# Three edits to the order of work in an attention and expert kernel: context halves, the first weight, the gate products

## The chip, the cores and the metric

The kernel runs on one core of one Trainium2 chip. The metric is the device time of one execution in microseconds (us), lower being better. The engines are named as the profile names them: PE is TensorE (matmuls; its weight loads are PEld), DVE is VectorE, ACT is ScalarE, POOL is GpSimd, and SP is the engine that issues nearly all DMAs. Each works through its own list in order and waits on semaphores.

## What is computed

The reference is cross attention followed by a layer of experts, each with a residual:

```python
x = x + _L0_xattn_ref(_layernorm(x, axis=-1), ctx_2048, ...)
x = x + _L0_ffn_ref(_layernorm(x, axis=-1), ...)
```

x is 4 batches of 512 rows of 512 numbers, and the context is 4 batches of 1601 rows of 512 (257 image rows and 1344 text rows, each kind with its own key and value weights). The attention has 16 heads of 32:

```python
q = rms_norm(linear(x, q_w, q_b), norm_q_w)
k = rms_norm(linear(ctx_txt, k_w, k_b), norm_k_w)
v = linear(ctx_txt, v_w, v_b)
k_img = rms_norm(linear(ctx_img, k_img_w, k_img_b), norm_k_img_w)
v_img = linear(ctx_img, v_img_w, v_img_b)
out = attention(q, k_img, v_img) + attention(q, k, v)
return linear(out, o_w, o_b)
```

The second part routes each of 2048 tokens to 4 of 32 experts and adds a shared gated layer, `silu(x @ shared_gate.T) * (x @ shared_up.T) @ shared_down.T`.

## The kernel before, in words

The order of every engine's list is written by hand, one block of code for each engine. There are two programs in a row: the attention, and then the feed-forward part. All engines meet between them.

**Precision.** Matmuls of the projections work on halves: a number of 32 bits is stored as a high half (a 16-bit copy) and a low half (the rest). Three products (high by high, high by low, low by high) make one `product` (line 900), which is 4 chunks by 3 = 12 matmuls of 512 columns. For the context tile k, ACT makes the high half (`ctx_high`, line 493) and DVE the low half (`ctx_low`, line 634). For a weight, ACT makes the high half (`weight_high`, line 489) and DVE the low one (`weight_low`, line 629), each in one instruction over 2048 columns. The semaphores `c_lo` and `w_lo` tell PE that they are there.

**A batch.** Each of the 4 batches has a projection stage of 17 slots (`project`: 13 context tiles for keys and values, 4 tiles of x for queries) and an attention stage of 52 steps. In slot i PE does the key (or query) product of tile i, transposes the normalised key of slot i - 2 (`turn_keys`), and does the value product of tile i - 1. DVE takes the key out of PSUM (`key_raw`, line 648), ACT squares it and sums (`key_square`, line 511), POOL makes the scale (`key_scale`), DVE normalises (`key_norm`, line 661), and ACT and DVE split it (`key_high`, `key_low`). The end of a batch is folded into the projection of the next one. In slots 1 to 4 PE spreads the reciprocal of the softmax sums over the heads (`spread`, line 975, into the banks NUM and DEN) and DVE multiplies with it (`weigh`, line 699); after that come the output product and the norm of the rows of the batch before.

**The change of batch.** PE does the key and the value product of tile 0 of the next batch (`key(bb + 1, 0)`, `value(bb + 1, 0)`), then the last sums of the softmax (`text_part`, line 1118, semaphore `a_den`). DVE has taken out key 0 by then, waits for `a_den` and computes the reciprocal (line 827, semaphore `a_rcp`). Only then does it go into the slots of the next batch, where the low half of context tile 1 stands first. SP waits for `a_den` before it loads x, two residual tiles and then context tile 2.

**The start.** SP first issues the image key weight WKI, context tile 0, the image value weight WVI, context tile 1, two vectors, the text weights WK and WV, and two more vectors. ACT and DVE split WKI, then tile 0, and then WVI; PE begins when all this but WVI is there.

**The end of the attention program.** After the last batch PE waits for the reciprocal and spreads it for head group 0 (line 1176). DVE sums up the reciprocals, PE adds the sum over the rows (line 1188), and DVE sets a flag (line 890) that says whether an exact second pass (never taken with these inputs) is needed. Every engine reads the flag and branches. Then the feed-forward program begins. Its PE list (from line 1811) starts with `spread` for groups 1 to 3, `gate_up(0)` (the gate product and the up product, 12 matmuls each, of the first block of normed rows, x2t[0]), `gate_up(1)`, and the four output products of the last batch. SP has begun to load x2t[0], [1] and [2] after the last scores (line 346, semaphores `s_turned`).

The names `wts`, `hl`, `raw`, `rcp`, `sel`, `x2t`, `sg` and `su` in the rows are weights in halves, context in halves, context as loaded, the reciprocal, the spreading matrices, the normed rows turned, and the shared gate and up weights. Rows of a DMA stand under the line of the call that issues it.

## Time and profile before

| | us |
|---|---|
| median of 3 runs | 1297.05 (1296.89 to 1299.68) |
| the profiled execution | 1295.91 |
| its span in the trace | 1294.1 |
| PE busy | 1203.9 (93%) |
| DVE busy | 865.9 (67%) |
| ACT busy | 676.7 (52%) |
| POOL busy | 186.6 (14%) |

The attention program takes the first 921 us and the feed-forward program the rest. The busy shares are a mean over stages: in most of the span PE works without a gap, and what an edit is worth is read at the places where PE doesn't. A timeline row gives the start and the time in us, the engine, the line, the operation, out<-in, the shapes and the count; the brackets behind it give the idle time of the engine just before and what ended it. A matmul of 32-bit operands (the spreading) leaves two records for one instruction. Starts of matmuls that follow on each other are closer than their durations, so a row of many ends a little later than the next one begins; times of stretches are taken from start to start.

### The profile page before, as it was taken

How to read it: one execution, taken by the hardware profiler on the slowest of the kernel's cores; microseconds unless marked ns; L12 is line 12 of the kernel's file. 1: busy time of each engine (PE TensorE's matmuls, PEld its weight loads, DVE VectorE, ACT ScalarE, POOL GpSimd, SP SyncE). 2: the span in 40 equal slices, each digit the busy share in tenths (PEclk: the TensorE clock that was granted, in tenths of full speed). 3: DMA queues.
4: the chain of work that ended last, by engine and by line, in shares of the span. 5: the costliest groups of instructions: out<-in, count | busy, mean ns of one | idle time of the engine just before them, and what ended most of it. 6: DMA issues, size and time to landing. Idle time of an engine off the chain costs nothing. (4 is left out here: it accounts for less than half of the span.)

```text
span 1294.1 us, 22341 instructions
## 1 busy us (share of the span) xinstructions
PE 1203.9 (93%) x9252; PEld 462.7 (36%) x9252; DVE 865.9 (67%) x1102; ACT 676.7 (52%) x944; POOL 186.6 (14%) x299
## 2 busy tenths in 40 slices
PE   5998999899899989989998998999799999999996
PEld 2543222355322234532223454222254434333332
DVE  6775888787588878758887885899658963122111
ACT  4546998345699924568993455899231111111121
POOL 0210000123000003300000230000120001333342
PEclk9999999899999989999999999999799999999999
DMA  8200000213100021210002123010561325999832
GB/s 301 85 25 18 2 2 2 90 33 108 41 2 2 2 85 39 90 58 2 2 2 82 36 95 139 2 34 2 200 261 66 123 82 201 364 309 304 262 68 30
DMA packets 38398, 117.95 MB, mean 91 GB/s; under 512 B 6544, under 2 KB 6800, under 8 KB 33040
## 3 DMA queue, kind: packets, MB, share of 16 engines
q1 hardware_dynamic: 33168, 105.60, 22.8%
q0 software_dynamic: 5120, 10.82, 4.6%
q8 instruction: 76, 1.25, 0.4%
q14 instruction: 34, 0.28, 0.1%
HBM read 95.67 MB, written 20.73 MB: 90 GB/s over the span
## 5 line engine op out<-in xcount | busy, mean ns | idle before, releaser
L597 ACT ACTIVATE work<-ps 128x1024 f32<-128x1024 f32 (+1 forms) x416 | 403.2, 1021 | 45.2 <-PE ps L1080 41.5
L1086 PE MATMUL ps<-work,vals 128*32 128x512 f32 (+2 forms) x1664 | 221.0, 603 | 0.9 <-ACT work L597 0.6
L903 PE MATMUL ps<-wts,work 128*128 128x512 f16 x864 | 203.7, 388 | 12.1 <-DVE work L636 12.1
L1080 PE MATMUL ps<-quer,keys 32*128 32x512 f16 x2496 | 171.9, 377 | 23.3 <-ACT work L597 9.3
L818 DVE TENSOR_TENSOR work<-work 128x2048 f32<-128x2048 f32 x64 | 146.6, 2291 | 6.0
L818 DVE TENSOR_TENSOR attn<-attn,work 128x2048 f32<-128x2048 f32 x62 | 142.0, 2291 | 5.2
L903 PEld LDWEIGHTS ps<-wts,work 128*128 128x128 f16 x864 | 83.7, 99 | 112.1 <-DVE work L636 14.8
L903 PE MATMUL ps<-wts,hl 128*128 128x512 f16 x480 | 111.9, 385 | 11.4 <-DVE hl L636 11.2
L1880 PE MATMUL ps<-wring,xgt 128*80 128x512 f32 x256 | 114.9, 592 | 0.0
L1080 PEld LDWEIGHTS ps<-quer,keys 32*128 32x128 f16 x2496 | 46.3, 92 | 191.6 <-ACT work L597 166.7
L1706 DVE COPY xgt<-ps 128x320 f32<-128x320 f32 x32 | 15.7, 492 | 138.4 <-PE ps L1871 138.4
L435 POOL TENSOR_SCALAR small<-small 128x1 f32<-128x1 f32 x68 | 13.7, 202 | 614.2 <-ACT work L514 614.2
L514 ACT ACTIVATE work<-work 128x512 f32<-128x512 f32 x68 | 42.9, 631 | 110.2 <-DVE work L653 110.2
L666 DVE SCALAR_TENSOR_TENSOR work<-work,small,vec 128x512 f32<-128x512 f32 (+1 forms) x72 | 63.6, 883 | 43.7 <-POOL small L438 43.6
L509 ACT CAST work<-work 128x512 f16<-128x512 f32 x68 | 42.1, 619 | 79.7 <-DVE work L666 79.7
L1453 ACT ACTIVATE yf<-ps,xg 80x512 f32<-80x512 f32 x32 | 21.9, 684 | 115.3 <-DMA out<-yf,idx 92.2
L1895 PE MATMUL ps<-wring,ht 128*80 128x512 f32 x128 | 62.2, 608 | 10.7 <-ACT ht L1448 8.9
L903 PEld LDWEIGHTS ps<-wts,hl 128*128 128x128 f16 x480 | 46.2, 99 | 68.1 <-issue 19.0
L802 DVE COPY nums<-ps 128x512 f32<-128x512 f32 x16 | 11.1, 692 | 81.0 <-PE ps L1086 81.0
L1086 PEld LDWEIGHTS ps<-work,vals 128*32 128x32 f32 (+2 forms) x1664 | 34.3, 107 | 85.7 <-issue 81.2
L1374 POOL DMA_INDIRECT out<-yf,idx x32 | 45.6, 1424 | 133.0 <-DMA out<-yf,idx 84.7
L1880 PEld LDWEIGHTS ps<-wring,xgt 128*80 128x80 f32 x256 | 38.4, 150 | 71.1 <-issue 70.9
(219 smaller groups left out, 1515.8 us busy)
## 6 DMA issues: line engine op xcount, KB each, us to landing
wring<-in_wx SPq DMA_DIRECT2D x32, 1536.0 KB, 8.9
raw<-in_ctx SPq DMA_DIRECT2D x52, 256.0 KB, 2.8
work<-in_x SPq DMA_DIRECT2D x4, 1024.0 KB, 5.6
table<-nums SPq DMA_DIRECT2D x16, 256.0 KB, 2.3
work<-in_x SPq DMA_DIRECT2D x12, 256.0 KB, 4.4
x<-work SPq DMA_DIRECT2D x12, 256.0 KB, 2.0
x2t_rows<-nums SPq DMA_DIRECT2D x12, 256.0 KB, 2.4
x2t<-x2t_rows SPq DMA_DIRECT2D x3, 1024.0 KB, 7.8
```

What stands on the lines that cost most here:

```text
L509: act.copy(stack[i % 2][:, 0, :], kraw[i % 2]).then_inc(k_hi, 1)
L514: act.activation(junk, kraw[i % 2], ACT.Square, accum_out=ssq[i % 2]).then_inc(k_sq, 1)
L597: act.activation(prob[0:rows, s % PROBS, 2 * half:2 * half + 2, :], ps[0:rows, 2 * pair:2 * pair + 2, :], ACT.Exp, scale=SCALE).then_inc(a ...
L666: ins = dve.scalar_tensor_tensor(kraw[i % 2][a:z, :], kraw[i % 2][a:z, :], rin[i % 2][a:z, :], vec[a:z, weight, :], ALU.mult, ALU.mult)
L818: dve.tensor_tensor(acc, acc, cur, ALU.add).then_inc(a_sum, 1)
L903: mm = pe.matmul(out, lhs(a, c)[:, cols], wts[:, w, z, c * D:(c + 1) * D], start=(k == 0), stop=(k == len(steps) - 1))
L1080: mm = pe.matmul(ps[:, 2 * pair + h % 2, :], k[h * HD:(h + 1) * HD, :], q[h * HD:(h + 1) * HD, :], start=(e == 0), stop=(e == len(terms) - 1))
L1086: return pe.matmul(ps[h * HD:(h + 1) * HD, NUM, :], vals[a:z, ORDER[n], g * P + h * HD:g * P + (h + 1) * HD], prob[a:z, s % PROBS, h, :], ...
L1374: pool.indirect_dma_start(out=out[:, :], out_offset=bass.IndirectOffsetOnAxis(ap=idx[:, n:n + 1], axis=0), in_=yf[n % 2][:, :], in_offset= ...
L1453: act.activation(yf[n % 2][:, :], ps[0:CAP, 2 + n % 2, :], ACT.Copy, scale=xg[n % GATHERS][:, D + n:D + n + 1]).then_inc(m_yf, 1)
L1880: mm = pe.matmul(ps[0:CAP, 7 if n % 2 == 0 else 0, :], xgt[n % 2][:, c, :], wring[n % RING][:, c * D:(c + 1) * D], start=(c == 0), stop=(c ...
L1895: mm = pe.matmul(ps[0:CAP, 2 + n % 2, :], ht[n % 2][:, c, :], wring[n % RING][:, (NC + c) * D:(NC + c + 1) * D], start=(c == 0), stop=(c = ...
```

## The change

**At each change of batch.** The low half of context tile 1 of the next batch is made by DVE before it waits for `a_den` and computes the reciprocal, and not after it. SP loads context tile 2 as soon as the low half of tile 0 is made, before it waits for `a_den`, and not behind the loads of x and the residuals. In slot 0 the load of tile 2 and in DVE's list the low half of tile 1 are left out accordingly.

**At the start.** SP issues context tile 0 ahead of WKI. ACT and DVE split tile 0 first and then WKI in two pieces of 1024 columns; PE waits for the first piece before its first product and for the second one half way through it. For the first batch, ACT makes the high half of context tile 2 right behind that of WK, ahead of the first `key_square` and of WV, and DVE makes the low half behind the first `key_raw`, ahead of WV. Before, both stood in slot 1.

**At the end of the attention.** The 12 gate products of `gate_up(0)` move from the feed-forward program to the place between the last `text_part` and the wait for the reciprocal. Their result stays in bank 0, so the spreading uses other banks, the third spread of the feed-forward program waits for the first `weigh`, and the flag's sum goes to bank 2.

```diff
-SEL_BANK = [(0, 2), (1, 3), (4, 5), (6, 7)]
+SEL_BANK = [(4, 5), (1, 3), (6, 7), (4, 5)]
+GATE_BANK, FLAG_BANK = 0, 2
...
             def one_pass(p):
+                load_ctx(p * B, 0, 0)
                 load_weight(WKI)
-                load_ctx(p * B, 0, 0)
                 load_weight(WVI)
...
                 for bb, b in passes(p):
+                    if b > 0:
+                        sp.wait_ge(c_lo, kvn(bb, 0))
+                        load_ctx(bb, b, 2)
                     upto(sp, a_den, bb * NG)
...
-                        if k is not None and k + 1 < KT:
+                        if k is not None and k + 1 < KT and (b == 0 or k > 1):
                             sp.wait_ge(c_lo, kvn(bb, k - 1))
                             load_ctx(bb, b, k + 1)
...
+            def first_weight_high(p):
+
+                act.wait_ge(s_w[WKI], 16 * (p + 1))
+                for half in range(2):
+                    cols = slice(half * 2 * D, (half + 1) * 2 * D)
+                    act.activation(wts[:, WKI, 0, cols], wstage[WKI][:, cols], ACT.Copy, scale=WS).then_inc(w_hi, 1)
+
...
-                    if i + 1 in KV_AT:
+                    if i + 1 in KV_AT and (b > 0 or i != 1):
                         ctx_high(bb, KV_AT[i + 1])
...
                     if b == 0 and i == 0:
                         weight_high(p, WK)
+                        ctx_high(bb, 2)
...
                     if b == 0:
-                        weight_high(p, WKI)
                         ctx_high(bb, 0)
+                        first_weight_high(p)
                         weight_high(p, WVI)
...
-                    if i + 1 in KV_AT:
+                    if i + 1 in KV_AT and i != (0 if b > 0 else 1):
                         ctx_low(bb, KV_AT[i + 1])
...
                     if b == 0 and i == 0:
+                        ctx_low(bb, 2)
                         weight_low(p, WV)
...
                 if b + 1 < B:
                     key_raw(bb + 1, 0)
+                    ctx_low(bb + 1, 1)
                 dve.wait_ge(a_den, (bb + 1) * NG)
...
             def product(out, lhs, w, cols=slice(0, P), halfway=None):
                 steps = [(c, a, z) for c in range(NC) for a, z in PARTS]
                 for k, (c, a, z) in enumerate(steps):
+                    if halfway is not None and k == len(steps) // 2:
+                        pe.wait_ge(w_lo, halfway)
...
                 if b == B - 1:
+                    pe.wait_ge(s_turned[0], 16 * (p + 1))
+                    pe.wait_ge(f_wlo, 3 * p + 1)
+                    steps = [(c, a, z) for c in range(NC) for a, z in PARTS]
+                    for k, (c, a, z) in enumerate(steps):
+                        pe.matmul(ps[:, GATE_BANK, :], swt[SG][:, a, c * D:c * D + P], m.x2t[0][:, :, z, c, :],
+                                  start=(k == 0), stop=(k == len(steps) - 1))
                     pe.wait_ge(a_rcp, bb + 1)
...
                 image, text = SEL_BANK[g]
+                if g == 3:
+                    pe.wait_ge(t_mt, 1)
...
-                for w, bank in ((SG, n % 2), (SU, 2 + n % 2)):
+                for w, bank in ((SG, n % 2), (SU, 2 + n % 2))[1 if n == 0 else 0:]:
```

How the lists read at the places of the prediction follows; the words in brackets are the semaphores that a row waits for. DVE at the first change of batch, before:

```order
L818 TENSOR_TENSOR attn<-attn,work 128x2048 [waits a_sum]
L653 SCALAR_TENSOR_TENSOR work<-ps,vec 128x512 [waits k_mm]
L827 RECIPROCAL rcp<-ps 128x512 [waits a_den]
L636 TENSOR_TENSOR work<-raw,work 128x512 [waits c_hi]
L666 SCALAR_TENSOR_TENSOR work<-work,small,vec 128x512 [waits k_rin]
L636 TENSOR_TENSOR work<-raw,work 128x512 [waits c_hi]
L672 TENSOR_TENSOR work<-work 128x512 [waits k_hi]
L653 SCALAR_TENSOR_TENSOR work<-ps,vec 128x512 [waits k_mm]
```

The same place now (the lines have moved: 636 is 660, 666 is 690, 827 is 853):

```order
L843 TENSOR_TENSOR attn<-attn,work 128x2048 [waits a_sum]
L677 SCALAR_TENSOR_TENSOR work<-ps,vec 128x512 [waits k_mm]
L660 TENSOR_TENSOR work<-raw,work 128x512 [waits c_hi]
L853 RECIPROCAL rcp<-ps 128x512 [waits a_den]
L690 SCALAR_TENSOR_TENSOR work<-work,small,vec 128x512 [waits k_rin]
L660 TENSOR_TENSOR work<-raw,work 128x512 [waits c_hi]
L696 TENSOR_TENSOR work<-work 128x512 [waits k_hi]
L677 SCALAR_TENSOR_TENSOR work<-ps,vec 128x512 [waits k_mm]
```

One row has moved from behind the reciprocal to ahead of it. ACT at the start of the program, before (`s_w3` is the arrival of WKI, `s_w4` WVI, `s_w1` WK, `s_w2` WV; `s_raw0` and `s_raw1` are the arrivals of context tiles):

```order
L491 ACTIVATE wts<-nums 128x2048 [waits s_w3]
L496 CAST hl_60<-raw 128x512 [waits s_raw0]
L491 ACTIVATE wts<-nums 128x2048 [waits s_w4]
L496 CAST work<-raw 128x512 [waits s_raw1]
L491 ACTIVATE wts<-quer 128x2048 [waits s_w1]
L514 ACTIVATE work,small<-work 128x512 [waits k_raw]
L491 ACTIVATE wts<-attn 128x2048 [waits s_w2]
L496 CAST work<-raw 128x512 [waits s_raw0]
```

The same place now:

```order
L511 CAST hl_60<-raw 128x512 [waits s_raw0]
L502 ACTIVATE wts<-nums 128x1024 [waits s_w3]
L502 ACTIVATE wts<-nums 128x1024
L506 ACTIVATE wts<-nums 128x2048 [waits s_w4]
L511 CAST work<-raw 128x512 [waits s_raw1]
L506 ACTIVATE wts<-quer 128x2048 [waits s_w1]
L511 CAST work<-raw 128x512 [waits s_raw0]
L529 ACTIVATE work,small<-work 128x512 [waits k_raw]
L506 ACTIVATE wts<-attn 128x2048 [waits s_w2]
```

The first weight is in two rows behind tile 0, and the cast of tile 2, which waits for its own load, stands ahead of the square (line 514, now 529) and of WV. PE at the end of the attention program, before:

```order
L1121 MATMUL ps<-attn,ones 32x512 [waits a_sum]
L1121 MATMUL ps<-attn,ones 32x512 x3
L1176 MATMUL ps<-rcp,sel 128x512 [waits a_rcp]
L1176 MATMUL ps<-rcp,sel 128x512
L1188 MATMUL ps<-small 1x1 [waits f_chk]
```

The same place now:

```order
L1150 MATMUL ps<-attn,ones 32x512 [waits a_sum]
L1150 MATMUL ps<-attn,ones 32x512 x3
L1207 MATMUL ps<-x2t_76,sg 128x512 [waits f_wlo,s_turned0]
L1207 MATMUL ps<-x2t_76,sg 128x512 x11
L1211 MATMUL ps<-rcp,sel 128x512 [waits a_rcp]
L1211 MATMUL ps<-rcp,sel 128x512
L1223 MATMUL ps<-small 1x1 [waits f_chk]
```

Twelve matmuls stand where PE had only a wait; the feed-forward program has twelve less ahead of its first up product.

## Rows read from the trace of the kernel before

**Rows 1.** Timeline of PE, DVE and ACT around the first change of batch.

```profile
216.10 0.69 DVE L636 TENSOR_TENSOR hl<-raw,hl 128x512 f16<-128x512 f32 x1
...
230.60 3.36 DVE L827 RECIPROCAL rcp<-ps 128x512 f32<-128x512 f32 x1 [1.02 <-PE ps L1121]
...
233.88 0.63 DVE L636 TENSOR_TENSOR work<-raw,work 128x512 f16<-128x512 f32 x1
...
234.56 5.30 PE L903 MATMUL ps<-wts,work 128*128 128x512 f16 x12 [4.03 <-DVE work L636]
238.14 0.62 ACT L496 CAST work<-raw 128x512 f16<-128x512 f32 x1 [7.80 <-DMA raw<-in_ctx]
...
241.93 2.78 PE L912 MATMUL ps<-wts,work 128*64 128x512 f16 x24
...
249.60 0.69 DVE L702 TENSOR_TENSOR nums<-nums,ps 128x512 f32<-128x512 f32 x1 [1.35 <-PE ps L983]
```

**Rows 2.** Busy times by window: engines in order, then granted clock, DMA share, GB/s.

```profile
234.60:242.00 7.40, 7.40 (x18) 2.76 (x20) 2.46 (x4) 2.42 (x6) 0.38 (x2) 0.60 0.58 206
```

**Rows 3.** Timeline: the second and third change of batch.

```profile
460.23 3.36 DVE L827 RECIPROCAL rcp<-ps 128x512 f32<-128x512 f32 x1 [1.02 <-PE ps L1121]
...
469.27 1.88 PE L983 MATMUL ps<-rcp,sel 128*128 128x512 f32 x4
...
471.08 2.78 PE L912 MATMUL ps<-wts,work 128*64 128x512 f16 x24
...
689.39 3.36 DVE L827 RECIPROCAL rcp<-ps 128x512 f32<-128x512 f32 x1 [1.02 <-PE ps L1121]
...
699.45 2.78 PE L912 MATMUL ps<-wts,work 128*64 128x512 f16 x24
```

**Rows 4.** Timeline of PE: the first scores after the first and second change.

```profile
340.78 0.83 PE L1080 MATMUL ps<-quer,keys 32*128 32x512 f16 x12 [0.21 <-ACT vals L504]
...
569.94 0.83 PE L1080 MATMUL ps<-quer,keys 32*128 32x512 f16 x12 [0.21 <-ACT vals L504]
```

**Rows 5.** DMA issues at 5.45 us and 10.58 us: size, us to landing.

```profile
vec<-in_kw SPq DMA_DIRECT2D x1, 256.0 KB, 14.0
...
raw<-in_ctx SPq DMA_DIRECT2D x1, 256.0 KB, 9.6
```

**Rows 6.** Timeline of ACT at the start, and of PE at 75 us.

```profile
19.05 0.63 ACT L514 ACTIVATE work<-work 128x512 f32<-128x512 f32 x1 [2.96 <-DVE work L653]
...
19.68 1.90 ACT L491 ACTIVATE wts<-attn 128x2048 f16<-128x2048 f32 x1
...
75.08 0.61 PE L962 MATMUL ps<-ident,work 128*128 128x128 f16 x8 [1.71 <-DVE keys L683]
```

**Rows 7.** Waits of DVE from 20 to 76 us: total, times, longest.

```profile
DVE work L666 <- POOL small L438: 9.3, 8, 1.7
DVE wts L631 <- ACT wts L491: 2.6, 1, 2.6
DVE work L672 <- ACT work L509: 1.4, 2, 0.7
```

**Rows 8.** DMA issue of x2t[0] at 908.42 us, in the columns of Rows 5.

```profile
x2t<-x2t_rows SPq DMA_DIRECT2D x1, 1024.0 KB, 5.5
```

**Rows 9.** Timeline: the end of the attention and the start of the feed-forward.

```profile
917.08 3.78 PE L1176 MATMUL ps<-rcp,sel 128*128 128x512 f32 x4 [3.48 <-DVE rcp L827]
...
921.02 0.15 DVE L890 TENSOR_SCALAR flag<-ps 1x1 int32<-1x1 f32 x1 [2.10 <-PE ps L1188]
...
926.60 2.05 PE L1738 MATMUL ps<-rcp,sel 128*128 128x512 f32 x2 [5.61 <-PEq L159]
...
933.54 2.75 PE L1733 MATMUL ps<-x2t,sg 128*128 128x512 f16 x12
...
938.75 0.69 DVE L1489 TENSOR_TENSOR attn<-nums,attn 128x512 f16<-128x512 f32 x1
...
943.90 10.52 PE L1733 MATMUL ps<-wts,attn 128*128 128x512 f16 x48
```

More of the change, by code:

```diff
@@ L282, in added, with weights @@
             return (bb * NG + g) * ADDS + a + 1 - PRODUCT_SUMS * (bb // B)
+        def weights(p, k):
+            return 7 * p + k + 1
         def rows_of(n):
@@ L627, in own, with first_weight_low @@
                 return dve_steps[0]
+            def first_weight_low(p):
+                for half in range(2):
+                    cols = slice(half * 2 * D, (half + 1) * 2 * D)
+                    dve.wait_ge(w_hi, 7 * p + half + 1)
+                    dve.scalar_tensor_tensor(wts[:, WKI, 1, cols], wstage[WKI][:, cols], WS, wts[:, WKI, 0, cols],
+                                             ALU.mult, ALU.subtract).then_inc(w_lo, 1)
             def weight_low(p, w):
-                dve.wait_ge(w_hi, 6 * p + W_ORDER.index(w) + 1)
+                dve.wait_ge(w_hi, weights(p, W_ORDER.index(w) + 1))
                 dve.scalar_tensor_tensor(wts[:, w, 1, :], wstage[w], WS, wts[:, w, 0, :], ALU.mult,
@@ L859, in one_pass @@
                     if b == 0:
-                        weight_low(p, WKI)
                         ctx_low(bb, 0)
+                        first_weight_low(p)
                         weight_low(p, WVI)
@@ L889, in _ @@
             dve.wait_ge(f_sum, 1)
-            dve.tensor_scalar(flag[:, :], ps[0:1, XTURN, 0:1], SAFE, 0.0, ALU.is_le, ALU.is_equal).then_inc(f_flag, 1)
+            dve.tensor_scalar(flag[:, :], ps[0:1, FLAG_BANK, 0:1], SAFE, 0.0, ALU.is_le, ALU.is_equal).then_inc(f_flag, 1)
             dve.wait_ge(f_flag, 1)
@@ L898, in _, with product @@
             PARTS = ((0, 0), (0, 1), (1, 0))
-            def product(out, lhs, w, cols=slice(0, P)):
+            def product(out, lhs, w, cols=slice(0, P), halfway=None):
                 steps = [(c, a, z) for c in range(NC) for a, z in PARTS]
                 for k, (c, a, z) in enumerate(steps):
+                    if halfway is not None and k == len(steps) // 2:
+                        pe.wait_ge(w_lo, halfway)
                     mm = pe.matmul(out, lhs(a, c)[:, cols], wts[:, w, z, c * D:(c + 1) * D],
@@ L922, in key @@
                     if bb % B == 0:
[L923 removed]
+                        pe.wait_ge(w_lo, 7 * (bb // B) + 1)
                 if i >= 2:
@@ L937, in key @@
                     if bb % B == 0:
-                        pe.wait_ge(w_lo, 6 * (bb // B) + 3)
+                        pe.wait_ge(w_lo, weights(bb // B, 3))
                     mixed(bank, ctx_lhs(k), WK, WKI).then_inc(k_mm, 1)
                 else:
-                    product(ps[:, bank, :], ctx_lhs(k), WK if k > 2 else WKI).then_inc(k_mm, 1)
+                    product(ps[:, bank, :], ctx_lhs(k), WK if k > 2 else WKI,
+                            halfway=weights(bb // B, 1) if bb % B == 0 and k == 0 else None).then_inc(k_mm, 1)
             def value(bb, k):
@@ L989, in output @@
                     if q == 0:
-                        pe.wait_ge(w_lo, 6)
+                        pe.wait_ge(w_lo, weights(0, 6))
                 if j < 2:
@@ L1187, in _ @@
             pe.wait_ge(f_chk, 2 * B + 2)
-            pe.matmul(ps[0:1, XTURN, 0:1], total, one, start=True, stop=True).then_inc(f_sum, 1)
+            pe.matmul(ps[0:1, FLAG_BANK, 0:1], total, one, start=True, stop=True).then_inc(f_sum, 1)
             pe.wait_ge(f_flag, 1)
```

13 lines of the change are left out of this document (5 added, 8 removed).

## The prediction

> **What bounds the kernel now.** I read the page first (PE busy 93% of the span), then PE's waits stage by stage, and then the timeline where PE stands still. In three of the places that the change touches PE is the engine that everybody waits for, and it loses time there itself: at each change of batch it stands 4.03 us until the low half of context tile 1 is made, which DVE does behind its reciprocal of 3.36 us [rows 1]. The key product behind this wait then takes 234.56 to about 239.7, 5.1 us for 12 matmuls, where the same product on a warm engine takes 2.6 (12 of the 48 gate and up matmuls of rows 9, which run from 933.54 to 943.90, so 0.216 us each). The granted clock says why: its mean is 0.60 from 234.60 to 242.00 [rows 2], mostly the lower level of 1.2 GHz, after PE had been idle. Does time that is won there reach the end? The case has its own test. From the start of the reciprocal to the mixed key product (the first matmuls of slot 2) the first change takes 241.93 - 230.60 = 11.33 us and the second 471.08 - 460.23 = 10.85, 0.48 less [rows 1, 3]. The first scores of these batches come 340.78 - 230.60 = 110.18 and 569.94 - 460.23 = 109.71 after it, 0.47 less [rows 1, 3, 4]. So PE's list carries a gain of slot 2 whole to the attention.
>
> The first batch is another matter. There DVE never waits for PE from 20 to 76 us: its waits are for POOL and ACT alone, links of one chain (square, scale, normalise, split) that it is itself part of [rows 7], and PE waits for that chain, 1.71 us at 75.08 for a key that DVE stores [rows 6]. What delays this chain at its head moves the end; what hastens PE ahead of it doesn't.
>
> **Part 1, the changes of batch.** The low half of tile 1 (0.63 us on DVE) moves into the 1.02 us in which DVE waits for the sums, so it costs nothing; if ACT made the high half later it would delay the reciprocal. PE then does the key product right behind the sums, 2.6 us at full clock, and is done some 0.8 us before the reciprocal. It has the reciprocal 3.36 us after its start, with 0.05 us from engine to engine (DVE ends at 234.51, PE starts at 234.56 [rows 1]). The first spread takes 471.08 - 469.27 = 1.81 us on a warm engine [rows 3]. So the mixed key product can start 3.36 + 0.05 + 1.81 = 5.22 us after the start of the reciprocal. It needs tile 2 by then. Before, tile 2 was loaded behind x and two residuals, and ACT waited 7.80 us for it, until 238.14 [rows 1], 7.5 us after the reciprocal's start; so the moved low half alone would win little, and the earlier load is what the rest hangs on. Now it's loaded once the low half of tile 0 is made, at 216.8 [rows 1], 13.8 us ahead of the reciprocal: SP waits there for tile 0 only, and behind this wait stand only the loads that wait for the sums anyway. The load of tile 3 takes the old place of tile 2 and lands near 238, before DVE wants it at about 239. After the reciprocal DVE normalises key 0 (0.7) and makes the low half of tile 2 (0.65), done some 1.4 us after the reciprocal and 0.4 us before the spread ends. That is the tightest point. Gains: 11.33 - 5.22 = 6.11, 10.85 - 5.22 = 5.63, and for the third change (699.45 - 689.39) - 5.22 = 4.84 [rows 1, 3]. **Sum: 16.6 us.** Bounds: the idle time alone, 3 x (4.03 - 0.8) = 9.7, if the clock still fell; 17.5 if the spread took 1.5.
>
> **What is late next** in these slots is DVE. Before, it waited 1.35 us for the second spread at 249.60, that is 7.67 us after the mixed product began [rows 1]. That wait now ends at 230.60 + 5.22 + 7.67 = 243.5. Between the reciprocal (233.96) and there DVE has 14 operations of 0.63 to 0.74 us [rows 1], at a mean of some 0.65 from start to start 9.1 us, so it is ready at 243.1. It stays ahead by 0.4 us, and PE stays the bound.
>
> **Part 2, the start.** PE can begin about 2 us earlier, as the split of WKI is in pieces and tile 0 is ready before. But PE isn't the bound of the first batch. The chain's head is the square on ACT at 19.05 and then WV's high half at 19.68 [rows 6], on which DVE's low half and all keys behind it hang. Now the cast of tile 2 stands ahead of both, and it waits for its load. That load was issued at 10.58 and took 9.6 us, until 20.2; the vector issued before it, at 5.45, landed at 19.45 [rows 5]. The queue was full, so a load that is issued 4.7 us sooner, but still behind that vector, lands at about the same time. ACT then starts the cast at 20.2 and ends it at 20.85 (0.62 and the hop), and the square, due at 19.05, comes 1.8 us late. DVE's moved low half is off the chain in either place. **Cost: 1.8 us.** Bounds: 0, if the tile lands before WK's high half is done; and a gain of 2.1, PE's earlier start, if I am wrong about the chain.
>
> **Part 3, the end of the attention.** The 12 gate products need x2t[0], issued at 908.42 and there after 5.5 us, at 913.9 [rows 8]. PE is idle from 913.60 (917.08 less 3.48) [rows 9], so they run from about 914.0 to 916.6 under the reciprocal, which ends at 917.0. They take 12 x 0.216 = 2.6 us off the feed-forward's list, where PE runs without a gap from 933.54 to 943.90 and on into the output products [rows 9]. These need DVE's last low half, done at 939.44; PE would come at 941.3, so 1.9 us of cover are left and the gain is whole. The output products start the chain to the next norm, so it passes on. Besides, PE is no longer idle for 3.48 us before the first spread, so that takes 1.81 and not 3.78 us, and ends at 918.9. The flag's sum then waits for DVE, which was ready at 918.92 (921.02 less 2.10) [rows 9], and the flag comes 1.8 us earlier. From flag to feed-forward all engines read, branch and meet (5.61 us of PE's idle time), which just moves. The spread of group 3 waits for a `weigh` that is long done. **Sum: 2.6 + 1.8 = 4.4 us**, bounds 1.8 (the output products wait after all) and 5.
>
> **The sum.** 16.6 + 4.4 - 1.8 = 19.2 us. The profiled execution took 1295.91 us, so it would take 1276.7. The median of the runs lies 1.1 above it, so I forecast 1277.9. The experts at the end hang on the chain before and move with it.
>
> **Rivals.**
> - *Tile 2 lands early at the start.* If the load overtakes the vector, the loss goes: 1276.1, and with a gain of PE's head start 1274. Against it: in rows 5 the tile landed 0.7 us behind the vector, issued 5.1 us before it. The Trainium skill (DMA: Bandwidth & Descriptors, Queues, rings and completion order) says that completion isn't first in, first out for one issuing engine, since data descriptors carry no barrier. By that rule the time would be this rival's; the landings of rows 5 speak for order. Chance 0.14.
> - *DVE becomes the bound at the change of batch.* Its 14 operations have 0.4 us to spare; two of them wait for a half that ACT makes, which can add 0.7 each. Then each change wins 1.0 to 1.4 us less, 3 to 4 in all: 1281 to 1282. Chance 0.12.
> - *The gate products come too late.* If x2t[0] lands after the reciprocal, they stand in front of the spread, at low clock, 12 x 0.43 = 5.1 us. That eats the 4.4 us: about 1282.6. Against it: 913.9 in rows 8. Chance 0.07.
> - *Slower than before.* With the pauses gone, PE would be granted 1.2 GHz in part of the attention stages. Matmuls that took T us at full clock take 2T there. The 19.2 us are gone from T = 19.2, and it decides for slower by more than the margin from T = 22: with 30 us of such matmuls the time is 1277.9 + 30 = 1308. Against it: the clock is below full here only after PE's pauses [rows 2]. Chance 0.02.
> - *It doesn't do what it says:* the moved steps wait for something I missed, and two of the three changes win nothing: 1289. Chance 0.03.
>
> **How the numbers follow.** The forecast has 0.62, from 1275.5 to 1280. The range 1273.5 to 1282.5 takes in the early landing and the DVE rival, 0.88 at face value; each case is itself uncertain by some 2 us (the three runs lie 2.8 apart), which leaves a little over 8 in 10. The measurement tells 0.2%, 2.6 us, from no change. All cases but the slower one and a failure of several parts win more than that: faster 0.96, same 0.02, slower 0.02.
>
> **What would show it.** Right: PE's wait before the key product of tile 1 is gone; the mixed key product starts 5.2 us after each reciprocal; the granted clock stays full there; ACT waits at 16 to 20 us for context tile 2 and WV's high half starts near 21.5; the wait at 75 us is longer by about 2 us; gate products lie under the last reciprocal, and 12 matmuls are missing in the feed-forward. Wrong: DVE's `weigh` no longer waits for PE; WV's high half starts before 20; the first scores of the first batch come earlier, not later.

## The result: 13 us faster, 6 us less than forecast

| | before | changed |
|---|---|---|
| median of 4 runs, us | 1296.97 (1295.46 to 1299.68) | 1284.01 (1282.3 to 1285.85) |
| ratio (95% interval) | 1 | 0.9901 (0.9886 to 0.9916) |
| the profiled execution, us | 1295.91 | 1282.94 |
| its span, us | 1294.1 | 1281.1 |
| PE busy, us | 1203.9 (93%) | 1205.8 (94%) |

The forecast was 1277.9 and its range 1273.5 to 1282.5, so the time lies outside. The sign was right, and the places of the gain were right. A single execution can be slow as a whole, and ratios leave it out; below that is one run, of `d3_start_only` (6833.44 us). I go through the places in the order of the program.

**The changes of batch do what was forecast.** The same stretch as rows 1, in the changed kernel (start, duration, engine, line, operation, count, and idle time before it with what ended it):

```profile
230.09 0.68 DVE L660 TENSOR_TENSOR work<-raw,work 128x512 f16<-128x512 f32 x1
...
231.06 2.76 PE L931 MATMUL ps<-wts,work 128*128 128x512 f16 x12
231.19 3.36 DVE L853 RECIPROCAL rcp<-ps 128x512 f32<-128x512 f32 x1 [0.43 <-PE ps L1150]
...
234.70 1.95 PE L1012 MATMUL ps<-rcp,sel 128*128 128x512 f32 x4 [0.88 <-DVE rcp L853]
...
236.58 2.78 PE L940 MATMUL ps<-wts,work 128*64 128x512 f16 x24
...
244.26 0.69 DVE L726 TENSOR_TENSOR nums<-nums,ps 128x512 f32<-128x512 f32 x1 [1.05 <-PE ps L1012]
```

PE's wait of 4.03 us before the key product is gone; it now stands 0.88 us before the spread, for the reciprocal. The key product takes 2.76 us where it took 5.30, and the mixed product starts 236.58 - 231.19 = 5.39 us after the reciprocal. DVE waits 1.05 us for the second spread, so it isn't the bound. The window of this stretch (busy time of PE, PEld, DVE, ACT and POOL, granted clock, DMA share, GB/s) has the clock at full speed, where rows 2 had 0.60:

```profile
231.00:236.60 5.60, 4.72 (x22) 1.79 (x18) 5.32 (x5) 1.05 (x2) 0.74 (x2) 1.00 0.78 248
```

The first scores come 104.22, 104.23 and 104.23 us after the three reciprocals, against 110.18, 109.71 and 108.92 [rows 1, 3, 4]. That is 5.96 + 5.48 + 4.69 = 16.1 us. The reciprocals of the second and third change in the changed kernel, each with the first scores behind it:

```profile
456.49 3.36 DVE L853 RECIPROCAL rcp<-ps 128x512 f32<-128x512 f32 x1 [0.43 <-PE ps L1150]
...
560.72 0.83 PE L1109 MATMUL ps<-quer,keys 32*128 32x512 f16 x12 [0.21 <-ACT vals L519]
...
681.79 3.36 DVE L853 RECIPROCAL rcp<-ps 128x512 f32<-128x512 f32 x1 [0.43 <-PE ps L1150]
...
786.02 0.83 PE L1109 MATMUL ps<-quer,keys 32*128 32x512 f16 x12 [0.22 <-ACT vals L519]
```

The old times that this is measured from differ a little by trace: three kernels below that keep the old change of batch (c3, d3, d4) have 328.5, 327.4 and 328.4 us for the three together, where the kernel before has 328.8. So up to 1.4 of the 16.1 us can be the luck of one trace.

**The attention stages are longer.** From the first scores of a batch to the start of its reciprocal, behind the last sums, is work that the change doesn't touch (I call it the attention stage). It took 119.45 us for batches 1 and 2 and 115.36 for batch 3 before, and 121.08, 121.07 and 116.97 now: 4.9 us in all. Only batch 0 is unchanged (119.38 and 119.36). The loss is at the head of each stage. PE at the head of batch 1's, first before, then changed:

```profile
342.81 0.83 PE L1080 MATMUL ps<-quer,keys 32*128 32x512 f16 x12 [1.21 <-ACT work L597]
344.77 0.82 PE L1080 MATMUL ps<-quer,keys 32*128 32x512 f16 x12 [1.13 <-ACT work L597]
345.52 1.06 PE L1086 MATMUL ps<-work,vals 128*32 128x512 f32 x8
```

```profile
335.41 0.83 PE L1109 MATMUL ps<-quer,keys 32*128 32x512 f16 x12 [0.21 <-ACT vals L519]
337.45 0.83 PE L1109 MATMUL ps<-quer,keys 32*128 32x512 f16 x12 [1.21 <-ACT work L613]
339.40 1.38 PE L1109 MATMUL ps<-quer,keys 32*128 32x512 f16 x12 [1.13 <-ACT work L613]
340.71 1.94 PE L1115 MATMUL ps<-work,vals 128*32 128x512 f32 x8
```

The pauses are the same in both kernels: PE waits 1.21 and then 1.13 us for ACT's exponentials, since there are no older scores to work on yet. In the changed kernel the granted clock falls behind the second of them, and the same matmuls take longer, the eight of the last row nearly twice as long. The windows of the first 10 us, before and changed, and within the latter of the first 4 and the next 3 us:

```profile
340.78:350.78 10.00, 7.66 (x97) 1.98 (x98) 1.70 (x3) 7.75 (x8) 0.00 (x0) 1.00 0.01 2
```

```profile
335.41:345.41 10.00, 7.67 (x76) 1.97 (x80) 1.70 (x3) 6.69 (x7) 0.00 (x0) 0.83 0.00 1
335.41:339.40 3.99, 1.66 (x24) 0.46 (x25) 1.70 (x3) 3.01 (x4) 0.00 (x0) 1.00 0.01 2
339.40:342.42 3.02, 3.02 (x21) 0.68 (x25) 0.00 (x0) 2.46 (x3) 0.00 (x0) 0.52 0.00 0
```

The mean of 0.83 over 10 us is 3.4 us at the lower level, 1.2 GHz; work at half speed for 3.4 us loses 1.7, and the stages are 1.62 longer. PE's busy share doesn't show this: at the lower clock PE counts as busy. It even rose by 1.9 us in all.

**The start.** ACT, which rows 6 show before:

```profile
19.19 0.62 ACT L511 CAST work<-raw 128x512 f16<-128x512 f32 x1 [3.36 <-DMA raw<-in_ctx]
19.71 0.62 ACT L529 ACTIVATE work<-work 128x512 f32<-128x512 f32 x1
...
20.34 1.90 ACT L506 ACTIVATE wts<-attn 128x2048 f16<-128x2048 f32 x1
```

The cast waits 3.36 us for its load. Of the DMA issues, these are the vector issued at 5.1 us and the tile issued at 5.6 us (size, us to landing), which so landed at 18.4 and 19.1:

```profile
vec<-in_kw SPq DMA_DIRECT2D x1, 256.0 KB, 13.3
...
raw<-in_ctx SPq DMA_DIRECT2D x1, 256.0 KB, 13.5
```

WV's high half starts at 20.34 where it started at 19.68. The first scores of batch 0 come at 111.83, not 111.22: 0.6 us later.

**The end of the attention.** PE and DVE where rows 9 show them before, and first the reciprocal in the kernel before, which rows 9 don't show:

```profile
913.67 3.36 DVE L827 RECIPROCAL rcp<-ps 128x512 f32<-128x512 f32 x1 [0.93 <-PE ps L1121]
```

```profile
902.99 3.36 DVE L853 RECIPROCAL rcp<-ps 128x512 f32<-128x512 f32 x1 [0.93 <-PE ps L1150]
...
903.46 2.76 PE L1207 MATMUL ps<-x2t,sg 128*128 128x512 f16 x12 [0.54 <-DMA x2t<-x2t_rows]
906.40 1.98 PE L1211 MATMUL ps<-rcp,sel 128*128 128x512 f32 x4 [0.18 <-DVE rcp L853]
...
908.54 0.14 DVE L916 TENSOR_SCALAR flag<-ps 1x1 int32<-1x1 f32 x1 [0.29 <-PE ps L1223]
...
914.01 2.05 PE L1775 MATMUL ps<-rcp,sel 128*128 128x512 f32 x2 [5.50 <-PEq L160]
...
922.11 2.75 PE L1768 MATMUL ps<-x2t,su 128*128 128x512 f16 x12
...
929.88 2.32 PE L1768 MATMUL ps<-wts,attn 128*128 128x512 f16 x10
```

From the reciprocal to the flag it takes 908.54 - 902.99 = 5.55 us (7.35 before), to the first spread 5.47 more (5.58), and to the output products 15.87 more (17.30). The last is 1.43 less, not 2.6, because the spreads behind the meeting of the engines run longer at the lower clock. Changed, then before:

```profile
914.01:922.11 8.10, 8.10 (x12) 3.35 (x13) 6.08 (x11) 1.24 (x2) 1.25 (x8) 0.64 0.69 230
```

```profile
926.60:933.54 6.94, 6.94 (x13) 2.91 (x13) 5.15 (x9) 1.24 (x2) 1.25 (x8) 0.75 0.57 188
```

The sum of the trace: 16.1 (changes of batch) - 4.9 (attention stages) - 0.6 (start) + 3.3 (end of the attention) - 1.0 (from the output products to the end, 351.2 us where it was 350.2) = 12.9 us, but for rounding the whole difference of the spans, 13.0. The last term isn't the change's: over all traces of this study this stretch took 349.3 to 354.0 us in the six with the old end of the attention and 349.4 to 352.2 in the eight with the new one. Here too the clock has a part. In the trace of the changed kernel PE waits 1.91 us for ACT in the experts, and the granted clock of the window 1110:1120 is 0.83; in the trace of before it is 1.00 from 943 to 1260.

```profile
1113.42 2.80 PE L1930 MATMUL ps<-wring,ht 128*80 128x512 f32 x4 [1.91 <-ACT ht L1483]
```

### The profile page after: what moved, and what is told of

Its sections match the earlier page's. It is cut to its first block and busy times, and to the rows that moved or that the text cites. A ratio compares the mean times of both kernels' runs of the same rounds, so it can differ in the third digit from the quotient of the medians.

```text
span 1281.1 us, 22343 instructions
## 1 busy us (share of the span) xinstructions
PE 1205.8 (94%) x9252; PEld 461.9 (36%) x9252; DVE 865.3 (68%) x1103; ACT 676.6 (53%) x945; POOL 186.5 (15%) x299
## 5 line engine op out<-in xcount | busy, mean ns | idle before, releaser
L1115 PE MATMUL ps<-work,vals 128*32 128x512 f32 (+2 forms) x1664 | 223.6, 610 | 0.9 <-ACT work L613 0.6
L827 DVE COPY nums<-ps 128x512 f32<-128x512 f32 x16 | 11.1, 691 | 85.9 <-PE ps L1115 85.9
```

Source lines behind the costliest of these rows:

```text
L1115: return pe.matmul(ps[h * HD:(h + 1) * HD, NUM, :], vals[a:z, ORDER[n], g * P + h * HD:g * P + (h + 1) * HD], prob[a:z, s % PROBS, h, :], ...
```

## The experiments

The theory after these traces: the low clock at the head of the attention stages takes back 4.9 us, and comes of the two pauses there. Rivals: the scores are slow for some other reason and the clock only follows; or the difference to the forecast lies in the parts, each worth less than I said.

### The changed kernel again, fillers, and the change of batch alone

`c1_after_again` is the changed kernel once more, to see what repeats.

> The changed kernel once more, for another traced execution. Theory A (TensorE's clock): in the first trace the granted clock fell at the start of the second, third and fourth attention stage, and each took 121.1 us from its first scores to the next reciprocal instead of 119.45. It depends on when PE's pauses of 1.2 us fall, so another execution may show 119.45 in all three (they lie 225.3 us apart and fared alike), and then be about 4.9 us shorter. Theory B (the moved load and half lengthen the attention stage itself, at its end): 121.1 us in every execution at full clock or not. Median 1284 by both.

`c2_after_fill` gives PE work in the two pauses, matmuls whose result is never read (the bank is written anew later):

```diff
+                def keep_busy(n):
+                    for _ in range(n):
+                        pe.matmul(ps[:, NUM, :], ident[:, :], quer[:, 0, 0, :], start=True, stop=True)
+
                 scores(0)
+                if b > 0:
+                    pe.wait_ge(o_out, xn(out_batch(bb - 1), QT - 1))
+                    pe.wait_ge(n_out, xn(out_batch(bb - 1), QT - 1))
+                keep_busy(4)
                 scores(1)
+                keep_busy(4)
```

The two new waits are for readers of that bank.

> The changed kernel with two times 4 extra matmuls of 512 columns (0.216 us each) at the start of each attention stage, into a bank that is overwritten later, where PE waits 1.2 us for ACT behind the first and the second scores. Theory A: the granted clock stays full there, each attention stage takes 119.4 to 119.8 us, and the median falls by 3 to 5 us against the changed kernel, to 1279 to 1281. Theory B: the stages stay at 121.1 us and the median at 1284 or above.

`c3_before_fill` is the kernel before with the same fillers.

> The kernel before with the same extra matmuls. Its trace showed no fall of the clock at any attention start. Theory A: it wins at most 1 to 2 us in the median (where other executions than the traced one had a fall), 1295 to 1297. Theory B: no effect, 1297. If the extra matmuls themselves cost time, this run shows it: each 0.2 us of it 0.8 us in all.

`c4_changes_only` is the kernel before with only the edits at the changes of batch (the low half ahead of the reciprocal, the load ahead of the sums).

> The kernel before with the edits at the changes of batch alone (low half of tile 1 ahead of the reciprocal, tile 2 loaded early); start and end as before. By the prediction 16.6 us less, 1280.4. Theory A: 16.6 less up to 4.9 for the clock at three attention starts, so 1280.4 to 1285.3, and the mixed key product 5.4 us after each reciprocal starts. Theory B: 11.7 less, 1285.3, with attention stages of 121.1 us at full clock.

| | median, us (range, runs) | ratio (95% interval) | stages of batches 0 to 3 in the trace, us |
|---|---|---|---|
| c1_after_again | 1283.77 (1282.4 to 1284.64, 4) | 0.9896 (0.9881 to 0.9911) | 119.39, 119.48, 121.10, 117.01 |
| c2_after_fill | 1278.1 (1277.05 to 1280.33, 4) | 0.9852 (0.9835 to 0.9869) | 119.40, 119.47, 119.47, 115.37 |
| c3_before_fill | 1296.37 (1292.54 to 1299.33, 12) | 0.9985 (0.9972 to 0.9997) | 119.37, 119.45, 119.45, 115.34 |
| c4_changes_only | 1285.87 (1283.38 to 1289.91, 6) | 0.9914 (0.9897 to 0.9930) | 119.37, 121.10, 121.10, 116.98 |

PE at the head of batch 1's attention with fillers, and the window that answers to the one above:

```profile
336.17 1.04 PE L1191 MATMUL ps<-quer,ident 128*128 128x512 f16 x4
337.45 0.83 PE L1109 MATMUL ps<-quer,keys 32*128 32x512 f16 x12 [0.24 <-ACT work L613]
338.21 1.04 PE L1191 MATMUL ps<-quer,ident 128*128 128x512 f16 x4
339.40 0.82 PE L1109 MATMUL ps<-quer,keys 32*128 32x512 f16 x12 [0.16 <-ACT work L613]
340.16 1.07 PE L1115 MATMUL ps<-work,vals 128*32 128x512 f32 x8
...
335.41:345.41 10.00, 9.60 (x104) 2.60 (x105) 1.70 (x3) 7.74 (x8) 0.00 (x0) 1.00 0.01 2
```

The scores start at the same 337.45 and 339.40 as without fillers, since ACT sets these; what changes is the clock behind them. The stages are back at their old length, and the time goes from 1283.8 to 1278.1. Work that nobody needs makes the kernel faster, so the clock is the cause and not the consequence. The gain of 5.7 us in the median is more than the 3 to 5 that I expected and than the stages can give (4.9 at most); the traces of c1 and c2 are 3.7 us apart, 3.3 of it in the two stages that fell in c1. The rest isn't explained, and the intervals allow it to be scatter. On the kernel before, whose stages hadn't fallen in its trace, the fillers are worth 0.15%, just clear of nothing. The change of batch alone brings 11.1 us, about what 16.1 - 4.9 leaves (its median of 1285.87 is 0.6 above the range that I expected), with all three stages after it 1.6 us longer: the loss comes with this part, not with the start or the end.

It isn't certain from one execution to the next, though: c1 has the identical program and kept its stage of batch 1. Over all traces, those of the next sections included:

```
                                            stages traced   of them fallen
changes of batch in full, no fillers              12               8
  (changed kernel twice, c4)          of these, batch 0: 3 traced, 0 fallen
no change or a part of it, no fillers             20               2
  (before, d1, d2, d3, d4)
with fillers (c2, c3, e1, e2, e3, f1)             24               0
                     of these, behind the shortened change: 15 traced, 0 fallen
```

The Trainium skill (TensorE: Matmul & The Clock Gate, A second HAM failure mode: psum-queue depth-cycling) tells of a kernel in which short idle times between groups of matmuls let the clock go down and up again. The traces here agree with it: the clock fell behind pauses of 1.21 and 1.13 us, and never where fillers stood in them. Why the identical pauses fell 8 times of 9 behind the shortened change of batch and seldom in the other kernels, I can't settle. The Trainium skill (TensorE: Matmul & The Clock Gate, What's actually happening) says that the monitor is free-running and isn't reset when a kernel starts; that would fit with c1, but no run here tests it.

### The two halves of the change of batch, apart

`d1_low_half_only`, the kernel before with the one moved DVE step:

```diff
-                    if i + 1 in KV_AT:
+                    if i + 1 in KV_AT and (b == 0 or i > 0):
                         ctx_low(bb, KV_AT[i + 1])
...
                     key_raw(bb + 1, 0)
+                    ctx_low(bb + 1, 1)
                 dve.wait_ge(a_den, (bb + 1) * NG)
```

> The kernel before with the low half of context tile 1 ahead of the reciprocal, and tile 2 loaded where it was. Theory A (both edits are needed, the load is what the rest hangs on): tile 2 still lands 7.5 us after the start of the reciprocal, ACT and DVE split it by 8.9, so the mixed key product starts 8.9 to 9.0 us after it instead of 11.33, 10.85 and 10.06: 5.3 us in all, 1292. Rival: PE's 4.03 us wait was the whole matter, and each change wins 4 us or more: 1285 or less.

`d2_load_only`, with the early load alone:

```diff
+                    if b > 0:
+                        sp.wait_ge(c_lo, kvn(bb, 0))
+                        load_ctx(bb, b, 2)
                     upto(sp, a_den, bb * NG)
...
-                        if k is not None and k + 1 < KT:
+                        if k is not None and k + 1 < KT and (b == 0 or k > 1):
                             sp.wait_ge(c_lo, kvn(bb, k - 1))
                             load_ctx(bb, b, k + 1)
```

> The kernel before with tile 2 loaded early, and the low half of tile 1 behind the reciprocal as before. Theory A: PE still waits 4.0 us and does the key product at the lower clock, and DVE has tile 2 ready before that ends, so the mixed key product starts no earlier than before, 10 to 11.3 us after the reciprocal: 1296 to 1297, no change. Rival: what was won is the load alone, 1290 or less.

Medians 1297.04 and 1297.14 us (10 runs each), ratios 1.0007 (0.9996 to 1.0019) and 1.0007 (0.9994 to 1.0020) to 1296.16 of the kernel before beside them. Neither alone shows a gain; together, in c4, they win 11. PE at the first change in d1, then in d2:

```profile
230.35 2.76 PE L904 MATMUL ps<-wts,work 128*128 128x512 f16 x12
...
239.54 4.08 PE L913 MATMUL ps<-wts,work 128*64 128x512 f16 x23 [3.59 <-DVE work L636]
```

```profile
234.56 4.22 PE L906 MATMUL ps<-wts,work 128*128 128x512 f16 x12 [4.03 <-DVE work L639]
...
240.44 2.78 PE L915 MATMUL ps<-wts,work 128*64 128x512 f16 x24
```

In d1 the pause has only moved: the key product runs at full clock right behind the sums, but then PE stands 3.59 us for the low half of tile 2 (whose load lands as late as in rows 1) and the mixed product takes 4.08 us for 23 matmuls instead of 2.78 for 24. After the first reciprocal the mixed product starts 2.3 us sooner, at 9.05 us as expected, but the first scores come only 0.7 us sooner: most of the gain goes to the low clock in the mixed product. At the second change they come 0.3 us sooner and at the third 0.7 us later. My expectation for d1, 5.3 us and 1292, had left this out and was wrong by 5 us; the one for d2, no change, held. In d2 the old pause of 4.03 is still there, its three changes win 0.8 us together, and one of its four stages fell (121.08). Two waits, one behind the other, both had to go.

### The start alone and the end alone

`d3_start_only` is the kernel before with the edits at the start; `d4_end_only` is the kernel before with the gate products in front of the wait for the last reciprocal, and the banks that go with it. Their diffs are the corresponding hunks of the diff above.

> The kernel before with the three edits at the start alone. Theory A (the first batch hangs on the chain of DVE, ACT and POOL that the cast of tile 2 holds up): the first scores come at 111.8 instead of 111.2, 0.6 us later, as in the changed kernel's traces, though PE starts 2.2 us earlier; time 1297 to 1298. Rival: the head start of PE pays and the first scores come 2 us earlier, 1295.

> The kernel before with the gate products under the last reciprocal, and nothing else changed. By the prediction the four output products start 4.4 us earlier after the last reciprocal's start (30.23 us before, 25.8). The changed kernel showed 26.89, since the granted clock stayed at 1.2 GHz for two more of the spreads of the feed-forward. Theory A: 25.8 to 26.9, by where the clock rises; time 1292.7 to 1294. Rival: the whole 4.4 us are always lost to the clock, no change.

d3 measured 1297.51 us, ratio 1.0005 (0.9992 to 1.0018), as expected, though not by the 0.6 us at the start that I had named. d4 measured 1292.61, ratio 0.9973 (0.9961 to 0.9986), 3.5 us, as expected. ACT at the start of d3:

```profile
20.70 0.62 ACT L508 CAST work<-raw 128x512 f16<-128x512 f32 x1 [4.65 <-DMA raw<-in_ctx]
21.23 0.62 ACT L526 ACTIVATE work<-work 128x512 f32<-128x512 f32 x1
...
21.85 1.89 ACT L503 ACTIVATE wts<-attn 128x2048 f16<-128x2048 f32 x1
```

Here the tile landed at 20.7 and the first scores of batch 0 came at 113.28, 2.06 us later than before. That is the forecast's case. The list of loads is the changed kernel's, where the tile landed at 19.1 (13.5 us from issue to landing there, 15.1 here); in the four traces of the changed kernel with this list and order of halves (the first one, c1, c2, e2) the first scores came at 111.8. In every trace but those of e1 and f1, whose loads stand in another order, the first scores come 91.4 to 91.5 us after WV's high half starts, from 19.54 us in d4 to 21.85 in d3. So the term of the start was right in its mechanism, but its size is set by when this load lands, which differed by 1.6 us; why it landed later in d3, no run shows.

In d4 the last reciprocal to the output products took 26.62 us, 3.6 less than the 30.23 of before, and the stage of batch 0 fell for once (121.02). The end is worth about what the changed kernel showed, 3.3.

### Three edits on top of the fillers

`e1_fill_start`: WK is issued ahead of the two image vectors, and context tile 2 ahead of WV, once its buffer is free.

```diff
                 load_ctx(p * B, 0, 1)
+                load_weight(WK)
                 if p == 0:
                     load_vec(KB + 1, "kib", s_vi)
                     load_vec(KW + 1, "kiw", s_vi)
-                load_weight(WK)
+                sp.wait_ge(c_lo, kvn(p * B, 0))
+                load_ctx(p * B, 0, 2)
                 load_weight(WV)
...
-                        if k is not None and k + 1 < KT and (b == 0 or k > 1):
+                        if k is not None and k + 1 < KT and k > 1:
                             sp.wait_ge(c_lo, kvn(bb, k - 1))
                             load_ctx(bb, b, k + 1)
```

> The changed kernel with the extra matmuls of c2_after_fill, and at the start WK issued ahead of the two image vectors and context tile 2 ahead of WV, behind a wait for the low half of tile 0. If the head of the first batch's chain is the landing of WK (13.9 us) and then the wait for tile 2 (19.2), tile 2 now lands by 15 to 16, WK by 12.5, and the first scores come 2 to 2.5 us before those of the changed kernel (111.8), at 109.3 to 109.8; median 1275.6 to 1276.1 against 1278.1. Rival: WV or the text vectors, now 1 to 2 us later, hold the chain instead, and nothing or less than 0.5 us is won.

`e2_fill_flag`: 24 more such matmuls behind the sum for the flag, which PE works off while it waits for the flag, branches and meets the others.

```diff
+            for _ in range(24):
+                pe.matmul(ps[:, 3, :], ident[:, :], quer[:, 0, 0, :], start=True, stop=True)
             pe.wait_ge(f_flag, 1)
```

> The changed kernel with the extra matmuls of c2_after_fill, and 24 more (5.2 us at full clock) behind the sum for the flag, where PE stands still for 5.5 us between the two programs. If PE reads the flag while they run, the clock stays full in the spreads of the feed-forward, and the output products start 2 to 2.9 us earlier than in c2_after_fill; 1275.5 to 1276. Rival: PE reads the flag and branches only behind them, all engines wait for it, and the kernel is 3 to 5 us slower than c2_after_fill, 1281 to 1283.

`e3_fill_halves_back`: the halves of context tile 2 of the first batch stand in slot 1 again, behind WV, as before the change.

> The changed kernel with the extra matmuls of c2_after_fill, and the high and low half of tile 2 of the first batch back in slot 1, behind WV. Theory A (ACT's wait for that tile ahead of the square costs the 0.6 us): WV's high half starts at about 19.4 instead of 20.3, the first scores come at 110.9 to 111.2 instead of 111.8, and the median falls by 0.6 to 0.9, to about 1277.4. Rival: the later reads of the pieces cost it and the first scores stay at 111.8.

| | median, us (range, runs) | ratio (95% interval) | first scores of batch 0 | last reciprocal to output products |
|---|---|---|---|---|
| c2_after_fill | 1278.1 | 0.9852 (0.9835 to 0.9869) | 111.78 | 27.12 |
| e1_fill_start | 1274.76 (1274.35 to 1276.66, 5) | 0.9831 (0.9817 to 0.9844) | 110.92 | 26.58 |
| e2_fill_flag | 1274.78 (1272.98 to 1276.38, 5) | 0.9834 (0.9819 to 0.9849) | 111.77 | 24.90 |
| e3_fill_halves_back | 1277.52 (1275.92 to 1281.19, 4) | 0.9857 (0.9837 to 0.9878) | 111.09 | 26.40 |

Each set of runs has its own runs of the kernel before beside it, so kernels of different sets are compared by their ratios. By these the intervals of e1 and e2 overlap with that of c2, and neither is shown to be faster; what follows rests on the traces.

e2 settles the second loss. PE in its trace:

```profile
903.59 5.35 PE L1234 MATMUL ps<-quer,ident 128*128 128x512 f16 x24
910.04 1.10 PE L1786 MATMUL ps<-rcp,sel 128*128 128x512 f32 x2 [1.10 <-PEq L160]
910.97 1.02 PE L1787 MATMUL ps<-rcp,sel 128*128 128x512 f32 x2
...
923.04 2.32 PE L1779 MATMUL ps<-wts,attn 128*128 128x512 f16 x10
```

The spreads now run at full clock from the first one, and from there to the output products it takes 13.0 us instead of 15.87 (13.0 again in f1 below; 14.9 to 16.0 in the other traces with the new end and the shortened changes). Against the 17.30 of rows 9 that is the 2.6 us of the gate products and 1.7 of the clock. The first spread itself comes 0.9 us later (11.90 us after the reciprocal, 11.02 in the changed kernel), so the net is 2 us. Against c2, where the first spread comes 11.50 us after the reciprocal, it is 0.4 us later and the net 2.2.

e1 took the head start only in part. Its cast of tile 2 is at 15.12 and WV's high half at 17.61, 2.7 us ahead of the changed kernel's, but the first scores gain only 0.9 us: the next wait on a load has come in between. ACT in e1:

```profile
15.12 0.62 ACT L513 CAST work<-raw 128x512 f16<-128x512 f32 x1 [1.10 <-DMA raw<-in_ctx]
...
17.61 1.90 ACT L508 ACTIVATE wts<-attn 128x2048 f16<-128x2048 f32 x1
...
27.78 0.62 ACT L513 CAST hl<-raw 128x512 f16<-128x512 f32 x1 [2.56 <-DMA raw<-in_ctx]
```

The last row is tile 3, which stands behind more in the queue. I had expected the scores between 109.3 and 109.8. The median of e1 lies 3.3 us below that of c2, which is more than these 0.9 us can give. e3 brings the first scores back to 111.09, 0.7 us sooner, and its interval is that of c2: the early halves of tile 2 cost those 0.7 us in the trace, too little for the runs to tell. e3 also keeps PE's early start (its first matmul is at 8.80 us, at 10.69 before), and its first scores come at 111.09 where the kernel before has 111.22: the head start of 1.9 us wins 0.1 us at most, as the prediction had it.

### Fillers, start and flag together

`f1_fill_start_flag` is e1 and e2 in one kernel.

> The changed kernel with all fillers (4 behind each of the first two scores of an attention stage, 24 behind the flag's sum), WK ahead of the two image vectors, and context tile 2 ahead of WV at the start. No work of the reference is left out. The edit to the start alone brought the fillers' kernel from 1278.1 to 1274.76 us, the 24 fillers alone to 1274.78. Theory (the two are in different places and add up): 2 x 3.3 us below 1278.1, about 1271.5; first scores of batch 0 at 110.9 us, the four stages 119.4, 119.5, 119.5 and 115.4 us, and 25 us from the last reciprocal to the output products. Rival (the two medians differ from 1278.1 in good part by the scatter at the end, which varies by some 2 us from execution to execution): the traces show 0.9 us for the start and 2.2 us for the flag, so 1278.1 - 3.1 = 1275, no better than either alone by more than the interval.

Measured: 1272.9 us (1271.37 to 1277.47, 5 runs), ratio 0.9821 (0.9797 to 0.9845), the lowest median of the study, 1.8% below before. It lies between the two expectations, and its interval overlaps with those of e1 and e2, so the runs don't show that it beats either. Its trace is nearer the theory: a span of 1271.1 us, 5.8 less than c2's, with 2.1 at the start (first scores of batch 0 at 109.64), 2.2 between the last reciprocal and the output products (24.95 us), and 1.4 in the stretch to the end, which varies by itself. The start is better than e1's by 1.3 us with the same list of loads. ACT in f1:

```profile
14.62 0.62 ACT L513 CAST work<-raw 128x512 f16<-128x512 f32 x1 [0.80 <-DMA raw<-in_ctx]
...
26.56 0.62 ACT L513 CAST hl<-raw 128x512 f16<-128x512 f32 x1 [1.54 <-DMA raw<-in_ctx]
```

Tile 3 came 1.2 us sooner than in e1. So the gain of the start depends on the landings of an execution too.

## Where the prediction was right and where it failed

- **PE is the bound at the changes of batch, and time won there reaches the first scores.** Right: 5.96, 5.48 and 4.69 us. Forecast were 6.11, 5.63 and 4.84; the mixed product starts 5.39 and not 5.22 us after the reciprocal. The 0.17 lie in the spread: it starts 3.51 us after the reciprocal's start, where I took 3.36 + 0.05, and takes 1.88 to the next product, where I took 1.81. Right also that the moved low half alone wins little (d1), and that DVE keeps ahead, with 1.05 us where I had reckoned 0.4. That a gain of slot 2 comes whole to the first scores holds where the matmuls stay at full clock; in d1, where they didn't, 2.3 us became 0.7.
- **From the first scores the gain goes on to the end unchanged. This step failed.** It was never worked out. The test by which I carried the gain (0.48 against 0.47) ended at the first scores, and rows 4 end there too. Behind them the attention stages give back 4.9 of the 16.1 us, shown by c2, which only fills the pauses and gets the old lengths back.
- **The rival with the right mechanism** was the slower one: PE granted 1.2 GHz in part of the attention stages. I gave it 0.02 because the clock was below full only after PE's pauses, and didn't look whether these stages have any. They have two each, and in the trace of before they stood there with the clock still full. Its price was mis-sized as well: it was told only as a case of 22 us and more, where it is 1.6 us a stage. As a term of the sum, up to 3 x 1.7, it would have put the forecast near 1283.
- **The start.** Mechanism right, size off: 0.6 us, where 1.8 was forecast; d3 had 2.06. The landings kept their order, as I had said against the rival of an overtaking: the tile came 0.7 us behind the vector issued before it. But this vector itself landed 1 us sooner than in rows 5, at 18.4. In d3 it did too (18.5), and the tile came 2.2 us behind it. So WV's high half starts at 20.34 and not near 21.5, and the wait at 75 us grew by 0.3 us (2.02, rows 6 have 1.71), not by 2. The time from issue to landing isn't a fixed number, and one trace of it gave me a term to a tenth of a microsecond. Which of the two values a trace gives is luck as far as the runs tell: four had the 0.6 and one the 2.06.
- **The end.** The gate products lie under the reciprocal, though by 0.1 us only (they end at 906.22, it at 906.35, as x2t[0] came 0.54 us after PE was free), and the flag comes 1.8 us earlier, both as forecast. The term of 2.6 was worth 1.4, as the spreads behind the flag took 8.1 us and not 6.94. I had treated the spreads at 1.2 GHz as the same before and after. e2 shows the term whole once they run at full clock.
- **DVE as bound, gate products too late, a change that doesn't do what it says:** none came.
- **The 1.0 us from the output products to the end** is the spread between traces (in c3 the same stretch was 3.7 us longer than before's), not a step of the argument.

Put together: 19.2 - 0.5 (mixed product) + 1.2 (start) - 4.9 (stages) - 1.1 (end) - 1.0 (output products to the end) = 12.9 us, 13.0 but for rounding.

## What to carry to other kernels

When a change takes a pause of the matmul engine away, follow the granted clock beyond the place of the change: read each later stretch in which the engine waits a little and often, and price it once at half speed, even where it runs at full speed now. A gain is carried to the end only if every stage behind it has been looked at in that way. Where the cause was the clock, a few matmuls without use in the pause were here both the test and the cure.

Two waits in a row on the same engine have to go together: each of the two edits alone measured 1.0007, both together 0.9914.

## What was new about the hardware

- Two pauses of 1.21 and 1.13 us, with 0.8 us of matmuls between them, were enough for the clock to fall to 1.2 GHz, and it wasn't the same in each execution of the same program (c1: stage 1 kept, stages 2 and 3 fell). With eight matmuls of 0.22 us a stage in the pauses it stayed up in 24 stages of 24, of which 15 are of the kind where it fell 8 times of 9 without them.
- Matmuls queued ahead of a wait and a branch are worked off while PE's sequencer is on its way through them: the 24 fillers of e2 ran from 903.59 to 908.94, and the first spread came only 0.9 us later than in the changed kernel (0.4 later than in c2), against 5.35 us of added matmuls.
- The same list of loads at the start gave landings 1.2 to 1.6 us apart between executions (context tile 2 at 19.1 and 20.7 in the changed kernel and d3, the cast of tile 3 that waits for its load at 26.56 and 27.78 in f1 and e1).
